# Folding of the next layer's weights behind the next sequence's masks, one power by GpSimd for the inverse deviation, and a new order of steps

## The reference

```python
x = x + _layernorm(_L0_attn_ref(_layernorm(x), ...))      # a first attention, then
x = x + _layernorm(_L0_ffn_ref(_layernorm(x), ...))       # six layers of:
for i in range(DEPTH):                                    # DEPTH = 6
    x = attn_layer(shift_tokens(x), Wqkv[i], q_scale[i], k_scale[i], Wo[i]) + x
    x = ffn_layer(shift_tokens(x), ln_g[i], ln_b[i], W1[i], b1[i], W2[i], b2[i]) + x
...
def attn_layer(x, Wqkv, qs, ksc, Wo):                     # 16 heads of 64, windows of 32
    q, k, v = split(x @ Wqkv)
    q, k = l2norm(q) * qs, l2norm(k) * ksc                # then rotary tables
    return local_attention(q, k, v) @ Wo                  # own and previous window, softmax
def ffn_layer(x, g, bln, W1, b1, W2, b2):
    xn = (x - mu) / jnp.sqrt(var + 1e-05) * g + bln
    a, gate = split(xn @ W1 + b1)
    return a * gelu(gate) @ W2 + b2
```

## Time and profile before

| | us |
|---|---|
| median of 3 runs | 2136.09 |
| lowest, highest | 2131.37, 2141.48 |
| the profiled execution | 2145.36 |
| its span in the trace | 2143.6 |
| PE busy | 1885.3 (88%) |
| DVE busy | 1545.3 (72%) |
| POOL busy | 1100.1 (51%) |
| ACT busy | 919.2 (43%) |

### The profile page before, as it was taken

One profiled execution on the slowest core, in us unless ns is written; L12 is line 12 of the kernel. 1 busy time (PEld: TensorE's weight loads), 2 busy tenths in 40 slices (PEclk: granted clock), 3 DMA queues, 4 the chain that ended last, 5 costly groups with the idle time before them and its releaser, 6 DMA issues.

```text
span 2143.6 us, 47126 instructions
## 1 busy us (share of the span) xinstructions
PE 1885.3 (88%) x20040; PEld 812.5 (38%) x20040; DVE 1545.3 (72%) x2524; ACT 919.2 (43%) x1460; POOL 1100.1 (51%) x822
## 2 busy tenths in 40 slices
PE   5999965789999989999999899999999999999974
PEld 2333332334334434443344344433443344334421
...
DMA packets 91750, 131.42 MB, mean 61 GB/s; under 512 B 16242, under 2 KB 35856, under 8 KB 91536
## 3 DMA queue, kind: packets, MB, share of 16 engines
...
...
## 4 chain that ended last, share of the span: by engine, by line
PE 45%; DVE 26%; POOL 18%; issue 6%; ACT 2%; DMA 2%; SPq 1%; POOLq 0%; DVEq 0%; ACTq 0%
PE ps_z L1081 12%; DVE t L755 5%; POOL prob L493 5%; POOL prob L499 5%; PE ps_r L1003 5%; POOL prob L503 4%; POOL k_hat L489 4%; DVE pt L793 3%; PE ps_z L1074 3%; DVE n_tmp L719 2%; DVE n_tmp L717 2%; DVE t L675 2%; PE ps_s L1058 2%; DVE top L784 2%; PE ps_z L887 2%
## 5 line engine op out<-in xcount | busy, mean ns | idle before, releaser
L755 DVE TENSOR_TENSOR t<-ps_r,rot 128x1024 f32<-128x1024 f32 x384 | 453.7, 1207 | 61.6 <-PE ps_r L1003 55.3
L1003 PE MATMUL ps_r<-xs,w_qk_sb 128*128 128x512 f32 x768 | 426.6, 649 | 72.0 <-ACT sq L555 71.1
L493 POOL TENSOR_TENSOR prob<-prob,top 128x1024 f32<-128x1024 f32 x96 | 184.0, 1916 | 444.1 <-DVE top L784 444.1
L1081 PE MATMUL ps_z<-z,vo 128*128 128x512 f32 x768 | 355.5, 606 | 2.2 <-ACT z L577 2.2
L555 ACT ACTIVATE sq<-ps_r 128x512 f32<-128x512 f32 x384 | 229.5, 598 | 273.8 <-DVE t L755 273.7
L489 POOL TENSOR_TENSOR q_hat<-t 128x512 f32<-128x512 f32 x192 | 242.6, 1272 | 196.9 <-DMA t<-t 194.8
L489 POOL TENSOR_TENSOR k_hat<-t 128x512 f32<-128x512 f32 x192 | 242.3, 1278 | 35.3 <-DMA t<-t 35.3
L1074 PE MATMUL ps_z<-pt,xtk 32*128 32x512 f32 x1536 | 198.9, 632 | 63.4 <-DVE pt L793 40.1
L577 ACT ACTIVATE z<-ps_z 128x512 f32<-128x512 f32 x384 | 207.4, 598 | 77.4 <-PE ps_z L1074 76.7
L1003 PEld LDWEIGHTS ps_r<-xs,w_qk_sb 128*128 128x128 f32 x768 | 120.1, 192 | 300.3 <-ACT sq L555 199.7
L1081 PEld LDWEIGHTS ps_z<-z,vo 128*128 128x128 f32 x768 | 141.0, 191 | 183.9 <-issue 160.9
...
## 6 DMA issues: line engine op xcount, KB each, us to landing
...
z<-q_hat SPq DMA_DIRECT2D x128, 16.0 KB
...
```

The lines of the kernel that those rows point to most:

```text
L493: nc.gpsimd.tensor_tensor(s, s, top[:, (TT * u + n) % P_SLOTS, :].unsqueeze(2).to_broadcast([P, HEADS, 2 * WIN]), ALU.subtract).then_inc(l ...
L755: nc.vector.tensor_tensor(t12[:, slot, :, :], ps_r[n % 2][:, :].unsqueeze(1).to_broadcast([P, 2, SEQ]), rot[:, n // PAIRS, :, :], ALU.mult ...
L1003: nc.tensor.matmul(ps_r[n % 2][:, :], w_qk_sb[:, n, :], xs[:, seq, WIN:WIN + SEQ], start=True, stop=True).then_inc(projected.sem, 1)
L1081: ins = nc.tensor.matmul(ps_z[:, 0, :], vo[:, h, :], z[:, h, :], start=(h == 0), stop=False, skip_group_check=True)
```

## The change

Three things. First, the inverse deviation of the feed-forward: DVE's step rstd (one addition and eleven instructions of Newton's method, with one more for the half) becomes a step vkeep on DVE, which only adds the epsilon out of PSUM, and a step rstd on GpSimd, one instruction with the power -0.5 on 128x4. Second, vo no longer stands ahead of the scores. It stands between project 5 and project 6 of the newer unit and waits for mask 3 of the next sequence; the scores lose their wait for its copies, out 0 and sums 0 get one, and SyncE asks for its weights one sequence later, in the same pass as the feed-forward's. Third, all four tables are new: out 1 now stands between hid 0 and score 1, out 2 and out 3 between the first projections, the mean leads the pass, and nback and spread 0 stand side by side.

```diff
 TENSOR_STEPS = [
-    ("mix", 3, 2), ("project", 12, 1), ("project", 13, 1), ("sums", 2, 1), ("out", 0, 2), ("project", 14, 1),
...
+    ("spread", 1, 1), ("sums", 2, 1), ("xturn", 0, 1), ("mean", 0, 3), ("xturn", 1, 1), ("spread", 2, 1),
...
-                if seq == 1 and c == 0 and layer + 1 < DEPTH:
+                if seq == 2 and c == 0 and layer + 1 < DEPTH:
                     sp.wait_ge(vo_made.sem, vo_made.done(layer, 3))
                     load_vo(layer + 1)
...
+                elif kind == "rstd":
+                    pool.wait_ge(rstd_rows.sem, rstd_rows.at(u - 1))
+                    pool.wait_ge(var_kept.sem, var_kept.at(u))
+                    nc.gpsimd.tensor_tensor(v_rstd[:, :], v_sum[:, :], minus_half[:, 0:TT], ALU.pow).then_inc(rstd_made.sem, 1)
...
-                elif kind == "rstd":
-                    dve.wait_ge(rstd_rows.sem, rstd_rows.at(u - 1))
+                elif kind == "vkeep":
+                    dve.wait_ge(rstd_made.sem, rstd_made.at(u - 1))
                     dve.wait_ge(var_made.sem, var_made.at(u))
-                    nc.vector.tensor_scalar(v_sum[:, :], ps_r[1][:, 0:TT], LN_EPS, None, ALU.add).then_inc(v_newton.sem, 1)
-                    inverse_sqrt(v_sum[:, :], v_half, v_tmp, v_rstd[:, :], v_newton, u, rstd_made)
+                    nc.vector.tensor_scalar(v_sum[:, :], ps_r[1][:, 0:TT], LN_EPS, None, ALU.add).then_inc(var_kept.sem, 1)
...
             def make_vo(layer):
                 pe.wait_ge(vo_in.sem, vo_in.done(layer, 31))
-                pe.wait_ge(keyed.sem, keyed.at(layer * BATCH, 3) if layer else 0)
-                pe.wait_ge(masked.sem, masked.at(layer * BATCH - 1, TT - 1))
+                pe.wait_ge(masked.sem, masked.at(layer * BATCH, TT - 1) if layer else 0)
...
                     if n == 0:
                         pe.wait_ge(masked.sem, masked.at(u - 1, TT - 1))
-                        if layer:
-                            pe.wait_ge(vo_copied.sem, vo_copied.done(layer - 1, 3))
+                        pe.wait_ge(vo_copied.sem, vo_copied.done(layer_seq(max(u - 1, 0))[0], 3))
...
                 elif kind == "score":
                     pe.wait_ge(masked.sem, masked.at(u, n - 1) if n else masked.at(u - 1, TT - 1))
-                    pe.wait_ge(vo_copied.sem, vo_copied.done(layer, 3))
...
                 elif kind == "out":
                     if n == 0:
                         pe.wait_ge(z_copied.sem, z_copied.all(u, range(4 * TT - 4, 4 * TT)))
+                        pe.wait_ge(vo_copied.sem, vo_copied.done(layer, 3))
```

More of the change, by code:

```diff
@@ L73 @@
 TENSOR_STEPS = [
-    ("mix", 3, 2), ("project", 12, 1), ("project", 13, 1), ("sums", 2, 1), ("out", 0, 2), ("project", 14, 1),
-    ("nback", 0, 1), ("project", 15, 1), ("spread", 0, 1), ("xturn", 0, 1), ("mean", 0, 3), ("out", 1, 2),
-    ("spread", 1, 1), ("var", 0, 3), ("sums", 3, 1), ("spread", 2, 1), ("out", 2, 2), ("rows", 0, 3),
-    ("spread", 3, 1), ("out", 3, 2), ("nturn", 1, 1), ("vo", 0, 2), ("hid", 0, 3), ("score", 0, 1), ("hid", 1, 3),
-    ("score", 1, 1), ("hid", 2, 3), ("score", 2, 1), ("project", 0, 0), ("xturn", 1, 1), ("down", 0, 3),
@@ L79 @@
-    ("score", 3, 1), ("project", 1, 0), ("mix", 0, 1), ("project", 2, 0), ("project", 3, 0), ("project", 4, 0),
-    ("project", 5, 0), ("mix", 1, 1), ("project", 6, 0), ("project", 7, 0), ("sums", 0, 0), ("project", 8, 0),
-    ("mix", 2, 1), ("project", 9, 0), ("sums", 1, 0), ("project", 10, 0), ("nturn", 0, 0), ("project", 11, 0),
+    ("spread", 1, 1), ("sums", 2, 1), ("xturn", 0, 1), ("mean", 0, 3), ("xturn", 1, 1), ("spread", 2, 1),
+    ("sums", 3, 1), ("var", 0, 3), ("spread", 3, 1), ("out", 0, 2), ("rows", 0, 3), ("nturn", 1, 1), ("score", 0, 1),
@@ new lines @@
+    ("hid", 0, 3), ("out", 1, 2), ("score", 1, 1), ("hid", 1, 3), ("score", 2, 1), ("hid", 2, 3), ("score", 3, 1),
+    ("down", 0, 3), ("project", 0, 0), ("out", 2, 2), ("project", 1, 0), ("project", 2, 0), ("out", 3, 2),
+    ("project", 3, 0), ("project", 4, 0), ("mix", 0, 1), ("project", 5, 0), ("vo", 0, 2), ("project", 6, 0),
+    ("sums", 0, 0), ("project", 7, 0), ("mix", 1, 1), ("project", 8, 0), ("project", 9, 0), ("sums", 1, 0),
+    ("project", 10, 0), ("nturn", 0, 0), ("project", 11, 0), ("mix", 2, 1), ("project", 12, 0), ("project", 13, 0),
@@ L82 @@
+    ("mix", 3, 1), ("nback", 0, 0), ("spread", 0, 0), ("project", 14, 0), ("project", 15, 0),
 ]
 VECTOR_STEPS = [
-    ("flip", 3, 2), ("rotate", 10, 1), ("rotate", 11, 1), ("newton", 0, 1), ("rotate", 12, 1), ("rotate", 13, 1),
-    ("rotate", 14, 1), ("rotate", 15, 1), ("keyed", 0, 1), ("keyed", 1, 1), ("rstd", 0, 3), ("keyed", 2, 1),
-    ("keyed", 3, 1), ("gain", 0, 3), ("newton", 1, 1), ("gated", 0, 3), ("mask", 0, 1), ("max", 0, 1),
-    ("gated", 1, 3), ("mask", 1, 1), ("max", 1, 1), ("gated", 2, 3), ("mask", 2, 1), ("psum", 0, 1), ("max", 2, 1),
@@ L88 @@
-    ("rotate", 0, 0), ("flip", 0, 1), ("mask", 3, 1), ("rotate", 1, 0), ("max", 3, 1), ("psum", 1, 1),
-    ("rotate", 2, 0), ("rotate", 3, 0), ("flip", 1, 1), ("rotate", 4, 0), ("rotate", 5, 0), ("psum", 2, 1),
-    ("rotate", 6, 0), ("rotate", 7, 0), ("flip", 2, 1), ("psum", 3, 1), ("rotate", 8, 0), ("rotate", 9, 0),
+    ("keyed", 0, 2), ("rotate", 14, 2), ("rotate", 15, 2), ("keyed", 1, 2), ("keyed", 2, 2), ("vkeep", 0, 4),
+    ("keyed", 3, 2), ("gain", 0, 4), ("newton", 1, 2), ("mask", 0, 2), ("gated", 0, 4), ("max", 0, 2), ("mask", 1, 2),
@@ L101 @@
+    ("square", 10, 1), ("zcopy", 8, 2), ("zcopy", 9, 2), ("square", 11, 1), ("zcopy", 10, 2), ("zcopy", 11, 2),
+    ("nrows", 0, 1),
 ]
 GPSIMD_STEPS = [
[L103 to L106 removed]
```

36 lines of the change are left out of this document (19 added, 17 removed).

## The result

| | us | ratio to before, 95% interval |
|---|---|---|
| before, beside it | 2134.59 (2131.37 to 2141.48) | |
| after | 2110.02 (2103.22 to 2117.94) | 0.9882 [0.9837, 0.9927] |
| the profiled execution of after, its span | 2103.22, 2101.5 | |

A forecast was written before the change was run, and what follows sets the result against it. The bound alternates, DVE for half a pass and TensorE for the other. Steady passes 65, less 2 for late swaps, plus 6, 1 and 1 give 71 off the median 2136.1: 2065 us, range 2034 to 2126.

The forecast's parts named there:

- The loop and its bound: From project 1 to nback, TensorE's branch takes 27.3 us and DVE's 29.6, so TensorE waits 2.3 at nback.
- spread 0: Right behind nback with no projection between, it waits for ACT's copy: 0.85 us lost a pass.
- newton 0 at 6.1 us: Last piece of DVE's branch before nback, kept at its old 6.1 us because GpSimd's additions 8 to 11 fall beside it again.
- Rival A: DVE's branch is longer than walked, some 25 handoffs each 0.06 late, 1.5 us; gain halved, 2100 us; chance 0.20.
- rival B: GpSimd's additions miss newton 0 and 2 us of contention go: 32 us more gained, 2033; chance 0.08.
- Rival D: Waits gathered from project 13 to 14 lower TensorE's clock: 84 us lost, 2149; chance 0.10.
- part 1: Outs among the projections, and vo moved: 2.8 us gained a pass, 4.0 with vo, 65 over the steady stretch.
- The 2 us set aside for late swaps: vo's and the feed-forward's weight loads two swaps apart make GpSimd additions late: 2 us lost in all, range 0 to 8.
- vo: Between projects 5 and 6, about 2.2 of its 3.5 us delays rotation 6 and newton 0; gain 4.0 in such a pass.
- The power: Inverse deviation on GpSimd takes 0.9 us (bounds 0.73 and 2.93), hidden by out 0: cost in a pass 0.
- rival E: Late addition 15 and a dear GpSimd power miss rows by 4 us or more: 96 lost, 2161; chance 0.04.
- The ends: Last unit's softmax waits take outs 2 and 3, gain 6 us; last feed-forward gains 1; filling passes 1.

The follow-up runs named there:

- filling the long wait: Changed kernel plus eight idle products ahead of nback's wait: 2085.21 us, 0.975 of before; with four more ahead of spread 0's wait: 2085.91 us, 0.9768.
- the hold: Changed kernel with GpSimd holding addition 10 until newton 0 of the same unit is done: 2042.19 us, 0.9542 of before; in the kernel before: 2108.72, 0.986.
- after_again: The changed kernel itself, unedited, run again on another chip beside the kernel before: 2118.63 us, 0.9909 of before.

## Why the prediction was off

**The loop and its bound: right.** Two branches meet at nback, DVE's is the later one, the waits of projections 2 to 8 are gone, and spread 0 pays 0.69 for the copy (0.85 forecast). TensorE's own branch has small waits that I had not seen (project 13's 0.64 for square 11 is the longest); they lie ahead of the later wait and cost nothing.

**The term that failed first: newton 0 at 6.1 us.** newton 0 with its split was walked at 6.1. The mean of the old trace is already 6.3, and after the change it is 7.1 in the passes without vo (6.4 to 8.3 over all). The other terms of DVE's branch were nearly right: 1.23 to the first rotation, waits 1.05 (1.0 forecast), rotations and the rest 21.5 (21.1). So the branch is 31.0, not 29.6, in a pass without vo, and 33.2, not 31.8, with it. Over 21 passes that is 29 us: 18 of them newton 0, 8 the other operations, and the rest vo's delay, below. The prediction named the collision and then carried the old duration over, though the old one itself held two collisions (the earlier trace rows shows one). In the new order newton 0 starts when GpSimd is in the middle of a row of additions, and two to four instructions are hit, three or four in most passes. Why GpSimd is further behind there than before is not separated. Rival A had the size of this (1.5 us a pass), with the wrong reason (many small handoffs); rival B had the cause, but in the direction of a gain that needed a hold to come true.

**The second failure: the clock, at no cost in the forecast.** Rival D described it: the waits gathered at one place, the clock low behind them. Its weight of 0.10 rested on "the densest 3 us after are no worse" than those of before. That comparison stood on nback waiting 2.3 at most, with projections beside; it waits up to 3.1, with 0.69 right behind. D's price was too high (3.5 us of work at half speed in each pass, 84 us): the stretch from nback to the mean loses 1.1 to 2.4 us in 12 passes of 21, 21 us, most of it in projections 14 and 15, and filling the long wait won some 30 (24 to 34 by the four pairs of ratios). The rule of the Trainium skill that I weighed there (Perfetto Trace Analysis, section Matmul Optimizations: matmuls back to back in batches, since the engine's power follows its use) is borne out by these rows, 0.62 against 1.00.

The two failures hang together: the branch is long, so the wait is long, so the clock falls. 29 + 21 = 50 us of steady loss. The half from nback to project 1, once the clock's share is taken out, was 0.5 us a pass better than walked without vo and 0.5 worse with it, which gives 5 back. That leaves 45, and by 45 the steady part missed (19.8 in place of the 65 of part 1). The 2 us set aside for late swaps are not told apart in it.

**vo: mis-sized.** 2.2 of its 3.5 us were to delay the branch. The branch is 2.2 longer in these passes, but that is chance: DVE's waits in it grow from 1.05 to 4.07, by 3.0, and newton 0 is 0.7 shorter (6.5), since only two of its instructions are hit there. The gain in such a pass is 1.45, not 4.0, of the 2.55 missing 1.4 in the branch and 0.7 the clock. With the hold these passes take 69.2 against 73.0 before, 3.8 less.

**The power: right.** 1.02 us at 128x4 (0.9 taken from bounds of 0.73 and 2.93; the leaning on plain additions was weak, as they take 1.27 us at 128x512 and GpSimd's products of 128x1024 take 1.9, not twice as long), hidden everywhere but in the last unit, worth nothing, by two runs. Removing DVE's Newton steps freed DVE where it waits. This also settles rival E.

**The ends: right, as far as they can be told.** 8 us were forecast. Between the first projection and the first mean the changed kernel gains 3.1 (161.0 and 158.0), behind the last mean 6.5, together 9.6; in after_again it is 0.4 and 4.5. The other 12.8 between the profiled executions lie ahead of the first projection and are not the change's.

**What stays open.** Why the clock falls in one pass and not in another with the same waits: nback's wait was 1.72 in the pass of 1272 without a loss and 1.72 in that of 988 with one. With the hold the clock fell behind waits of 0.43, 0.72 and 0.88 at nback and not behind 0.60 and 0.75. The waits ahead of it may matter; no run separates them.
